# Rotated queries of the last stage: adding the two halves on VectorE, one product with the key-value sums on TensorE

## The reference

```python
q = gelu(x @ Wq.T + bq) + 0.21
q_r = _rope(q)                       # per pair: x1*cos - x2*sin, x2*cos + x1*sin
z = 1.0 / (einsum('bhnd,bhd->bhn', qh, kh.mean(axis=2)) + 1e-06)
out = einsum('bhnd,bhde->bhne', qrh, kv) * z[..., None]
res = out.reshape(b, n, c) + x
return (res - mu) / sqrt(var + 1e-12) * gamma + beta
```

## Time and profile before

| | us |
|---|---|
| median of 3 runs (lowest, highest) | 5882.93 (5879.49, 5885.64) |
| profiled execution | 5885.59 |
| its span, first to last instruction | 5883.5 |
| TensorE busy | 5145.9 |
| VectorE busy | 4283.5 |

### The profile page before, as it was taken

One profiled execution on the slowest core, in us unless ns is written; L12 is line 12 of the kernel. 1 busy time (PEld: TensorE's weight loads), 2 busy tenths in 40 slices (PEclk: granted clock), 3 DMA queues, 4 the chain that ended last, 5 costly groups with the idle time before them and its releaser, 6 DMA issues. The chain is left out here.

```text
span 5883.5 us, 80028 instructions
## 1 busy us (share of the span) xinstructions
PE 5145.9 (87%) x26286; PEld 3061.8 (52%) x26286; DVE 4283.5 (73%) x8723; ACT 2960.2 (50%) x6282; POOL 2998.5 (51%) x1603
## 2 busy tenths in 40 slices
PE   6788778777775899998999899999989989998877
PEld 2222222222231677776555566666655555556745
DVE  3999999999999798886333677777743337784249
ACT  4776776776774677774111455555521114342233
POOL 4999899899888455553111444444411100003724
PEclk9888998899886899999999999999999999999988
DMA  5565665556563222222111111111121134344565
GB/s 135 144 150 140 144 153 143 136 147 149 132 144 85 92 87 87 87 87 67 54 54 47 49 34 36 33 33 33 32 58 54 54 122 141 129 134 126 150 200 185
DMA packets 503856, 598.15 MB, mean 102 GB/s; under 512 B 59782, under 2 KB 381332, under 8 KB 499348
## 3 DMA queue, kind: packets, MB, share of 16 engines
q1 hardware_dynamic: 484308, 582.36, 36.0%
q10 hardware_dynamic: 6848, 8.67, 0.5%
q0 software_dynamic: 12288, 2.00, 0.3%
HBM read 429.38 MB, written 180.37 MB: 104 GB/s over the span
## 5 line engine op out<-in xcount | busy, mean ns | idle before, releaser
L654 POOL TENSOR_TENSOR db<-durep,brep 128x2048 f32<-128x2048 f32 x256 | 1161.0, 4535 | 188.8 <-DVE p_h L561 178.2
L513 ACT ACTIVATE p_h<-dlrep,am 128x512 f32<-128x512 f32 x1024 | 704.5, 691 | 196.4 <-DVE hh L572 171.3
L561 DVE TENSOR_TENSOR_SCAN p_h<-p_h,hlast,db 128x512 f32<-128x512 f32 x576 | 720.2, 1283 | 0.0
L1213 POOL TENSOR_TENSOR rn<-n,mhalf 128x16 f32<-128x16 f32 x128 | 374.8, 2929 | 630.3 <-DVE n L1160 630.2
L349 PE MATMUL p_acc<-hh,fold 128*32 128x512 f32 x2048 | 316.5, 694 | 343.0 <-DVE hh L572 341.7
L572 DVE TENSOR_TENSOR hh<-p_h,crep 128x512 f32<-128x512 f32 x768 | 519.9, 677 | 0.0
L1538 POOL TENSOR_TENSOR grstd<-grstd,mhalf 128x4 f32<-128x4 f32 x32 | 32.6, 1018 | 788.2 <-DVE grstd L1465 788.2
L1217 POOL TENSOR_TENSOR rot_cos<-rot_cos,rot_sin 128x1024 f32<-128x1024 f32 x128 | 301.9, 2359 | 220.9 <-DVE rot_sin L1150 220.9
L946 PE MATMUL p_o<-probT,v 128*64 128x128 f32 x4096 | 407.4, 280 | 7.3 <-DVE probT L1133 3.9
L1030 ACT ACTIVATE probT<-p_t 128x512 f32<-128x512 f32 x256 | 152.7, 597 | 480.1 <-PE p_t L933 480.1
L946 PEld LDWEIGHTS p_o<-probT,v 128*64 128x64 f32 x4096 | 345.3, 137 | 91.0 <-issue 70.7
(11 more groups left out here) (277 smaller groups left out, 11926.8 us busy)
## 6 DMA issues: line engine op xcount, KB each, us to landing
dlrep<-delta_rows SPq DMA_DIRECT2D x256, 256.0 KB
durep<-drive_rows SPq DMA_DIRECT2D x256, 256.0 KB
ew<-in_L_ffn_w SPq DMA_DIRECT2D x192, 176.0 KB
first_queries_keys<-qs SPq DMA_DIRECT2D x128, 256.0 KB, 2.1
qk<-first_queries_keys SPq DMA_DIRECT2D x64, 512.0 KB, 3.8
brep<-bc_rows SPq DMA_DIRECT2D x64, 256.0 KB
crep<-bc_rows SPq DMA_DIRECT2D x64, 256.0 KB
delta_rows<-dl SPq DMA_DIRECT2D x64, 256.0 KB
```

The costliest lines, as they stand in the source:

```text
L513: act.activation(p_h[:, (i % BANKS) * CH:(i % BANKS + 1) * CH], dlrep[use % 2][:, j], ACT.Exp, scale=am[:, q, j, g:g + 1]).then_inc(s_ex, 1)
L561: dve.tensor_tensor_scan(out=state, data0=bank, data1=db[s % 2][:, j], initial=0.0 if first else hlast[:, i % TILES:i % TILES + 1], op0=AL ...
L654: pool.tensor_tensor(out=db[s % 2][:], in0=durep[use % 2][:], in1=brep[c % 2][:, g:g + 1, :].to_broadcast([P, 4, CH]), op=ALU.mult).then_i ...
L1213: pool.tensor_tensor(out=rn[f % 2][:], in0=n2[f % 2][:], in1=mhalf[:], op=ALU.pow).then_inc(s_rn, 1)
```

## The change

VectorE's `rotate` gets a third instruction: it waits until the two products are written, and then adds them into `rot[k][0]`. It is a `scalar_tensor_tensor` with the scalar 0.0, both inputs and the output in SBUF, 128x1024. `s_rot` now comes from this instruction. TensorE makes one matmul for each block of the product with `kv` in place of two.

```diff
+    s_half = sem("f_half")
@@ attend, TensorE
-                        for a in range(2):
-                            ins = pe.matmul(p_o[:, at:at + P], rot[k][a][:, f, j * P:(j + 1) * P],
-                                            kv[b % 2][:, f * P:(f + 1) * P], start=(a == 0), stop=(a == 1))
+                        ins = pe.matmul(p_o[:, at:at + P], rot[k][0][:, f, j * P:(j + 1) * P],
+                                        kv[b % 2][:, f * P:(f + 1) * P], start=True, stop=True)
@@ rotate, VectorE
-                ins.then_inc(s_rot, 1)
+                ins.then_inc(s_half, 1)
+                dve.wait_ge(s_half, f + 1)
+                dve.scalar_tensor_tensor(out=rot[k][0][:], in0=rot[k][0][:], scalar=0.0, in1=rot[k][1][:], op0=ALU.add,
+                                         op1=ALU.add).then_inc(s_rot, 1)
```

## The result

The changed kernel takes 5911.55 us (median of 5 runs, 5911.26 to 5915.92) against 5882.86 us for the kernel before (5 runs, 5873.78 to 5885.64). The ratio is 1.0053, with a 95% interval of 1.0041 to 1.0064. That is 28.7 us slower; 5917.1 was forecast, in a range from 5891 to 5923. A second set of runs on another occasion gave 5915.52 against 5884.39 us, ratio 1.0053 again (1.0039 to 1.0067), 31.1 us.

The account below looks back on a forecast made before the run. VectorE was taken as the bound in ten of the passes from 3 on. 32.7 + 1.34 - 0.12 + 0.40 - 0.07 = +34.2 us on the median of 5882.93 gave 5917.1 us, range 5891 to 5923.

Parts of the forecast that it names:

- the first case: In ten VectorE-bound passes the add stands behind GpSimd's running join, 3.27 us each; time 5917.1 us; chance 0.73.
- The deciding term: VectorE's add beside GpSimd's join: zz starts 3.27 us later per pass, of which 1.95 is standing.
- What no row had shown: A VectorE instruction with two SBUF inputs kept out by a long GpSimd instruction; assumed for the add, 1.95 us standing.
- Passes 6 and 10: Passes with waits for the product and L2441 standing behind the join: cost +1.34 us and -0.12 us.
- Sum over passes 3 to 14: Ten VectorE-bound passes at 3.27 us, 32.7 us together, plus +1.34 in pass 6 and -0.12 in pass 10.
- The upper bound of the term: Add beside the join: all 2.49 us of the join pass from its issue, then full 1.21 and gap; 3.45 us.
- Passes 1 and 2: No join beside the add; the removed wait for the product offsets it: -0.07 us and +0.40 us.
- TensorE: Halved product takes 1.8 us off its 12.22 per pass, worth nothing in VectorE-bound passes.
- The fifth case: TensorE, idle 5.6 us per pass, is clocked low throughout and becomes the bound; time near 5960 us; chance 0.04.

Follow-up runs that it names:

- The first experiment: Changed kernel, with GpSimd's join of a chunk first waiting for VectorE's add of the same chunk: 5898.33 us against 5879.72 us for the kernel before.
- the fourth: Changed kernel, with the add as a plain tensor_tensor without the scalar: 5917.59 us against 5879.72 us for the kernel before, ratio 1.0065.
- the sixth: Changed kernel, with GpSimd's join replaced by a memset of the same tile: 5894.60 us in one run, against a median of 5881.19 us before.
- the seventh: Changed kernel, with GpSimd's join made as two instructions of half the size: 5903.35 us against 5881.19 us for the kernel before, ratio 1.0037.
- the second experiment: Changed kernel, with TensorE making both products again: 5913.82 us, 34.1 over the kernel before, ratio 1.0057.

## Why the prediction was right

The direction, the engine and the mechanism were as forecast. The median, 5911.55, lies at the lower end of the first case's own range (5911 to 5923).

- **The deciding term.** Forecast: the add begins its work 0.14 us before the join's end, and zz moves by 3.27 us. Measured in pass 4: zz at T+5.55 against T+2.27, 3.28. The two parts of the 3.27 were each off by 0.07: the add is issued at T+2.38, not T+2.45, so its own price is 1.25 (a plain pass of 14.02 us beside the memset) and not 1.32, and it stands 2.03 us and not 1.95. The sum isn't touched by that, as it hangs on the join's end and not on when the add is issued. The first experiment shows the cause and its size (2.03 us of standing go with the join out of the way), the fourth that the form doesn't matter, the sixth that the join's reads do, and the seventh that the price is what is left of one GpSimd instruction.
- **What no row had shown** was an instruction with two SBUF inputs being kept out by GpSimd. It was argued from L2441 and L2482 standing, and from GpSimd standing behind the rotates. The changed kernel shows it directly, and so does the kernel without L2482. The rule of the Trainium skill's SBUF — State Buffer, "Who interferes with whom", on two SBUF inputs against a GpSimd instruction that reads, holds here for the long instructions: 3.25 us beside a join, 1.23 beside a memset. It doesn't for GpSimd's small power, which reads SBUF too: the rotate beside it keeps its 1.21 us, and the measurement decides.
- **Passes 6 and 10.** Forecast +1.34 and -0.12, measured +1.37 (15.39 to 16.76) and -0.08 (16.85 to 16.77). L2444, the former L2441, takes 0.17 us in both.
- **Pass 5** was not foreseen: 16.40 us in place of 16.05, with 0.46 us of idle time before L2468. It comes back at the same place in the kernels that have the add, by 0.3 to 0.4 us. Its cause is open.
- **Sum over passes 3 to 14.** Forecast 32.7 + 1.34 - 0.12 = 33.9, measured 34.41 us (S), of which pass 5 is 0.35. The upper bound of the term, 3.45, comes out at 3.51 from its own words (the join from T+2.06 for 2.49, then 0.10 and 1.21, zz 0.08 before the end); over ten passes that is 0.6 us.
- **Passes 1 and 2.** L2462, the former L2459, came at T+4.45 in place of 4.64 in pass 1 (-0.19, forecast -0.07) and at T+5.20 in place of 4.88 in pass 2 (+0.32, forecast +0.40). The loads' landing hides this: from the stage's first load to pass 3, 98.70 us became 99.88 and 99.45 in the two profiles.
- **TensorE.** Worth nothing under the new bound, as the second experiment shows. The fifth case was half there: the granted clock was 0.79 in pass 4 of the changed kernel, the product of 16 took up to 3.76 us against 2.03 in pass 2, and the queries behind it 7.74 in place of 7.03. So in such passes most of the halving was lost to the clock, and TensorE idled 3.57 us in pass 4 and not 5.6; but the pass still had room, and no L2462 waited for the product.

What was off is the median by 5.6 us. The stage itself grew by more than forecast (34.41 us in S, 1.18 ahead of it, 0.35 behind it), so the difference is not in a term of the sum. It lies in the seven stages ahead, where the same instructions came up to 9 us earlier in the changed kernel's profile, and where kernels without the add scatter as well. Whether the change has any part in that can't be told from these runs; as far as they show, it is chance that the time came out below the forecast and not above.

## What to carry to other kernels

Before an instruction with two SBUF inputs is added to VectorE, look at what GpSimd runs at that very moment: the price can be the rest of GpSimd's instruction on top of its own length. This kernel has a few windows into which GpSimd's long adds fit: the join ran beside zz, the reciprocal and the product with it, which read PSUM, and the residual beside the moments' reductions, and none of these was longer for it; a new instruction, or an existing one, should be shifted against them, or the GpSimd instruction cut in parts. And read the first passes of a stage on their own: the largest gain here was not in the steady passes but in one load that stood behind a wait in its queue.

## What the runs showed of the hardware

- The turn passes per instruction: with GpSimd's join cut in two, the waiting VectorE instruction got in between (2.17 us in place of 3.25).
- GpSimd's small power (128x4) doesn't keep VectorE out for its 1.02 us. It waits for the first rotate and is recorded until 5703.57, and yet the second rotate beside it takes its plain 1.21 us, in all passes.
- A dependent VectorE instruction isn't always 0.10 us behind its predecessor: the add starts 0.03 us after the rotates' end (5712.04 and 5712.07), where L2468 starts 0.09 to 0.10 after L2462.
- TensorE did less and was clocked lower. In the last stage its busy time fell by 1.9 us only (217.85 to 215.98), where sixteen halved products at full pace would have saved 29.3; the granted clock of the stage went from 0.88 to 0.77. The view by windows gives busy us by engine, then the granted clock; first the kernel before, where TensorE didn't idle from 5700 to 5730, then pass 4 of the changed kernel, where it idled 3.57 us ahead of L2338, as its timeline behind it shows:

```profile
5700.00:5730.00 30.00, 30.00 (x168) 21.46 (x168) 28.95 (x59) 13.01 (x15) 17.84 (x9) 1.00 0.78 244
```

```profile
5709.00:5725.00 16.00, 12.43 (x46) 8.69 (x45) 15.54 (x25) 6.04 (x7) 6.68 (x4) 0.79 0.61 197
```

```profile
5715.60 2.81 PE L2338 MATMUL fp_z<-fkm,fqT 128*128 128x8 f32 x16 [3.57 <-DVE zz L2452]
5718.26 3.76 PE L2347 MATMUL fp_o<-fkv,frot 128*128 128x128 f32 x16
```

The first is the level of 2.4 GHz throughout, the second a mixture of 2.4 and 1.2 GHz.
